# One program part instead of four for MLP, experts, graph rows and second attention of a two-layer graph network

## What is computed

```python
xn = layernorm(x)
# layer 0: weighted graph sum, linear attention with an MLP behind it, experts
x = x + segment_sum((xn @ W)[src] * edge_w, dst) + mix0(xn)       # mix0 ends: gelu(gelu(ln(a) @ w1 + b1) @ w2 + b2) + a
x = x + ffn0(layernorm(x))                                        # 8 experts of width 64, top 2 of a router
# layer 1
xn = layernorm(x)
h = (xn * rsqrt(mean(xn ** 2) + 1e-6) * rms_w) @ W_down           # 1024 -> 256
xl, xr = h @ Wl, h @ Wr                                           # 256 -> 256, 4 heads of 64
e = einsum(leaky_relu(xl[src] + xr[dst]), att)                    # a logit per edge and head
graph = segment_sum(segment_softmax(e, dst) * xl[src], dst) @ W_up
mix1 = (phi(q) (phi(k)^T v) / den) @ Wo + bo                      # q, k, v: 1024 -> 1024, 16 heads, 266 random features
x = x + graph + mix1
x = x + ffn1(layernorm(x))                                        # shared expert and 16 routed experts, top 2
```

## Time and profile before

| | |
|---|---|
| runs of the kernel before | 2126.6 us median of 3 (2124.15 to 2135.53) |
| profiled execution, its own time | 2126.32 us |
| span of its trace | 2124.5 us |
| TensorE busy | 1958.2 us (92%), 9370 products |
| VectorE, ScalarE, GpSimd busy | 740.6, 390.2, 640.6 us |
| mean granted TensorE clock | 0.958 of full |

### The profile page before, as it was taken

How to read it: one execution, slowest core, us unless ns; L and a number is a source line. 1 busy time by engine, 2 the same in 40 slices (tenths; PEclk the granted TensorE clock), 3 DMA queues, 4 the chain that set the end, 5 groups by cost and what they waited for, 6 DMA issues and landing times. The chain is left out here.

```text
span 2124.5 us, 23644 instructions
## 1 busy us (share of the span) xinstructions
PE 1958.2 (92%) x9370; PEld 1310.7 (62%) x9370; DVE 740.6 (35%) x1462; ACT 390.2 (18%) x726; POOL 640.6 (30%) x566
## 2 busy tenths in 40 slices
PE   7999999999997999999889999999979999999962
PEld 6475446456455676457667766677448778877841
DVE  5964103335044133544444552402101222122126
ACT  0000000012001010005557632110012211221112
POOL 0667840300000676777884000005100001001000
PEclk9999999999999999998999999999989999999986
DMA  9553141636100334332221441503137988888833
GB/s 352 141 141 66 2 99 41 206 69 263 46 0 15 114 97 127 91 79 59 52 57 18 105 123 40 201 18 119 40 129 281 353 335 331 349 351 320 343 96 103
DMA packets 111649, 306.58 MB, mean 144 GB/s; under 512 B 65892, under 2 KB 68575, under 8 KB 99423
## 3 DMA queue, kind: packets, MB, share of 16 engines
q1 hardware_dynamic: 29822, 224.82, 29.3%
q0 software_dynamic: 69840, 57.84, 11.5%
q10 hardware_dynamic: 11906, 22.80, 3.3%
HBM read 272.00 MB, written 32.94 MB: 144 GB/s over the span
## 5 line engine op out<-in xcount | busy, mean ns | idle before, releaser
L1882 PEld LDWEIGHTS bank<-picked_t,wring 128*128 128x128 f32 x2560 | 291.5, 193 | 10.3 <-issue 9.1
L1882 PE MATMUL bank<-picked_t,wring 128*128 128x128 f32 x2560 | 291.7, 276 | 0.8 <-DVE picked_t L1925 0.8
L326 PE MATMUL bank<-wring,ln_buf 128*125 128x512 f32 x480 | 207.6, 593 | 1.6 <-DVE ln_buf L630 0.7
L513 POOL DMA_INDIRECT table_d<-wring x85 | 173.0, 2036 | 107.6 <-issue 76.7
L326 PEld LDWEIGHTS bank<-wring,ln_buf 128*125 128x125 f32 x480 | 89.5, 188 | 115.3 <-issue 114.3
L1901 PE MATMUL bank<-wring,unit_t 128*128 128x512 f32 x320 | 148.0, 605 | 7.1 <-DVE unit_t L1931 7.1
L342 PE MATMUL bank<-x_buf,wring 128*128 128x312 f32 (+1 forms) x512 | 136.4, 429 | 13.7 <-PEq L962 13.7
L2108 POOL DMA_INDIRECT routed_d<-out_rows,place_of x20 | 19.8, 990 | 407.5 <-DVE out_rows L1952 407.5
L1085 POOL DMA_INDIRECT score_d<-wring x90 | 117.3, 1303 | 73.7 <-DMA score_d<-wring 52.3
L342 PEld LDWEIGHTS bank<-x_buf,wring 128*128 128x128 f32 x512 | 97.6, 191 | 52.5 <-issue 15.0
L1071 POOL DMA_INDIRECT wring<-xr_d,wring x85 | 116.2, 1367 | 25.9 <-issue 24.7
(11 more groups left out here) (360 smaller groups left out, 2865.2 us busy)
## 6 DMA issues: line engine op xcount, KB each, us to landing
wring<-in_experts SPq DMA_DIRECT2D x60, 2048.0 KB, 9.4
wring<-in_L_Ws SPq DMA_DIRECT2D x6, 2048.0 KB, 24.7
b_b<-in_expert_b ACTq DMA_DIRECT2D x22, 512.0 KB, 13.7
table_d<-eq_buf SPq DMA_DIRECT2D x2, 3072.0 KB, 29.5
score_d<-no_edge SPq DMA_DIRECT2D x2, 3072.0 KB, 31.0
wring<-table_d POOLq DMA_DIRECT2D x10, 610.4 KB, 7.3
wring<-score_d SPq DMA_DIRECT2D x5, 1093.8 KB
wring<-pid_d ACTq DMA_DIRECT2D x17, 312.5 KB
```

Of the source, the lines that this page charges most:

```text
L326: ins = pe.matmul(bank[0:R, :], act_t[:, k, tok(t)], w[:, k * HALF:(k + 1) * HALF], start=(k == 0), stop=(k == chunks - 1))
L513: pool.indirect_dma_start(out=tables_d[b % 2], out_offset=bass.IndirectOffsetOnAxis(ap=edge_at[:, b:b + 1], axis=0), in_=edge_sums[:, b, : ...
L1882: ins = pe.matmul(bank[:, c * BLK:(c + 1) * BLK], w[:, k * HALF + c * P:k * HALF + (c + 1) * P], picked_t[:, s, k, :], start=(k == 0), sto ...
```

## The change

One block takes the place of the four. With no block ends between them, buffers are shared by hand (`flat_b`, `flat_c`, `flat_d`, `turned_a`), and the router's small tensors lie in free columns of weight slot 5. No `pe_keep_busy` is left in this part. What differs inside:
- **Norms by tile.** `dve_tile_var`, `act_tile_root` and `dve_tile_norm` do one row tile each; `pe_turn` transposes one row tile (8 transposes to one bank of each ring). The first tiles are normed between the last MLP tiles, the others between gate-up tiles; in the graph rows' norm tile t is normed after the second down tile of t.
- **Experts.** silu reads the gate-up bank in PSUM, VectorE multiplies from PSUM (no `gu`); the hidden rows are turned by tile. The logits come after the third gate-up tile.
- **Graph rows.** Instead of `g_t`, the weights in slot 5 are scaled by `rms_w` (8 pieces of 256 columns, during the experts). The mean square comes from the variance already there. Wl and Wr come after the first of the four column chunks of q (`ends`), and `xlr` is stored with four DMAs, of 112 and of 13 partitions for each table.
- **Logits.** VectorE does groups 0 to 4 during q and k, 5 to 8 after values tiles 1, 4, 6, 9, then one group in 10.5 units of the loop (`LATE_STEP_AT`); group 17 falls behind the loop. The maxima of row tiles 0 and 1 come before the adds of the Wo tiles, and `TURN_AT`, `ROWS_AT`, `FIND_AT`, `WEIGH_AT` start one tile later.
- **Queues.** SyncE: after the MLP loads 13 to 16, the score table clear, load 17, a wait for the end of the gate-up product, edge ends and `att`, a wait for `xlr`, the four stores, the other loads. GpSimd: `rank` and `no_edge` before its adds of x; then waits for the clear and for the stores before its constants and the gathers. ScalarE: the load of `gate8` moves ahead of the MLP.

```diff
-        with nc.Block() as block:      # experts: L878 to L948
-                pe_keep_busy(pe, 30)
-                pe.wait_ge(normed.sem, normed.n + T)
-                pe_transposes(pe, rows)
-                pe_wait_evacuated(pe)
-                pe_logits(pe, x_t, gate8, NE0)
-                pe_gemm_rows(pe, x_t)
-                pe_keep_busy(pe, 28)
...
-        with nc.Block() as block:      # graph rows: L962 to L1025
-                pe_keep_busy(pe, 24)
...
-                sp.dma_start(xl_d.rearrange("(t p) d -> p t d", p=R), xlr[:, :, 0:HID]).then_inc(scratch_out, 16)
-                sp.dma_start(xr_d.rearrange("(t p) d -> p t d", p=R), xlr[:, :, HID:]).then_inc(scratch_out, 16)
...
+        tile_order.insert(tile_order.index(("mlp", 2 * T - 1)), ("turn", 0))
+        tile_order.append(("turn", 1))
...
+        def pe_turn(pe, src, t, ready):
+            pe.wait_ge(normed.sem, ready)
+            for g, ring in ((0, dring), (1, sring)):
+                bank = ring.produce(pe)
+                for j in range(4):
+                    ins = pe.transpose(bank[:, tok(j)], src[:, t, (4 * g + j) * P:(4 * g + j + 1) * P], ident[0:R, 0:R])
+                ins.then_inc(ring.filled, 1)
...
+        def dve_tile_var(v, t, eps):
+            after(v, dve_step)
+            dve_step.mark(v.bn_aggr(mv[:, t, :], stats[:, t, :, :].rearrange("p h s -> p (h s)")))
+            after(v, dve_step)
+            v.tensor_scalar(var_eps[:, t:t + 1], mv[:, t, 1:2], eps, None, ALU.add).then_inc(ln_var, 1)
...
+        def act_tile_root(s, t):
+            s.wait_ge(ln_var, act_calls[0])
+            s.activation(root[:, t:t + 1], var_eps[:, t:t + 1], ACT.Sqrt).then_inc(ln_root, 1)
...
-        QK_GROUPS = 6
-        LOOP_GROUP_AT = 6
+        QK_GROUPS = 5
+        V_GROUP_AT = {1: 5, 4: 6, 6: 7, 9: 8}
+        LATE_GROUP = QK_GROUPS + len(V_GROUP_AT)
+        LATE_STEP_AT = {6 + 21 * g // 2 + 2 * n for g in range(GROUPS_E + 1 - LATE_GROUP) for n in range(4)}
...
-        TURN_AT = {1: 0, 3: 1, 5: 2, 7: 3, 8: 4}
-        ROWS_AT = {3: 0, 5: 1, 7: 2, 8: 3, 9: 4}
-        FIND_AT = {1: 2, 2: 3, 4: 4}
-        WEIGH_AT = {0: 1, 3: 2, 5: 3, 7: 4}
+        TURN_AT = {2: 0, 4: 1, 6: 2, 7: 3, 8: 4}
+        ROWS_AT = {4: 0, 6: 1, 7: 2, 8: 3, 9: 4}
+        FIND_AT = {2: 2, 4: 3, 6: 4}
+        WEIGH_AT = {0: 0, 1: 1, 3: 2, 5: 3, 7: 4}
...
+            @block.tensor              # gate-up in the one block
+                for h in range(2):
+                    w = wt.take(pe)
+                    for t in range(T):
+                        if h == 0:
+                            pe_wait_turned(pe, turned[t])
...
+                        if (h, t) == (0, 0):
+                            turned[2] = pe_turn(pe, rows, 2, LN_FFN + 3)
+                            turned[3] = pe_turn(pe, rows, 3, LN_FFN + 4)
+                        if (h, t) == (0, 1):
+                            turned[4] = pe_turn(pe, rows, 4, LN_FFN + 5)
+                        if (h, t) == (0, 2):
+                            pe_wait_turned(pe, turned[4])
+                            pe_logits(pe, x_t, gate8, NE0)
+                        if h and t:
+                            turn_hidden(t - 1)
...
+                pe_gemm_cols(pe, x1_t, ring=sring, beside=ends)
...
+            @block.vector              # last MLP tiles
+                    if n >= T + 2:
+                        dve_tile_norm(v, res, rows, n - T - 2, calls[n - T - 2])
+                    if n >= 1:
+                        add_output(n - 1)
+                    if n >= T + 1:
+                        calls[n - T - 1] = dve_tile_var(v, n - T - 1, 1e-5)
...
-                    if u >= LOOP_GROUP_AT and u % 2 == 0:
+                    if u in LATE_STEP_AT:
                         next(late, None)
-                    if TOP_AT <= u < TOP_AT + 2 * GH:
-                        find_top((u - TOP_AT) // GH, (u - TOP_AT) % GH)
-                assert next(late, "none") == "none"
+                for _ in late:
+                    pass
                 v.wait_ge(hsem["o_copied"], HEADS)
...
-                weigh(0)
+                find_tops(0)
+                find_tops(1)
...
+            @block.sync
+                sp.wait_ge(d_emptied, xlr_made[0])
+                for r0, n in ((0, 112), (112, R - 112)):
+                    for table, at in ((xl_d, 0), (xr_d, HID)):
+                        sp.dma_start(table.rearrange("(t p) d -> p t d", p=R)[r0:r0 + n],
+                                     xlr[r0:r0 + n, :, at:at + HID]).then_inc(scratch_out, 16)
```

More of the change, by code:

```diff
@@ new lines, in _ @@
+                mid_tiles = sring.made
+                turned = {}
+                for kind, n in tile_order:
+                    if kind == "agg":
+                        agg_tile(n)
+                        continue
+                    if kind == "turn":
+                        turned[n] = pe_turn(pe, rows, n, LN_FFN + n + 1)
+                        continue
+                    if n == 0:
+                        pe.wait_ge(s_emptied, mid_tiles)
+                    h, t = n // T, n % T
+                    bank = dring.produce(pe)
+                    pe.matmul(bank[0:R, :], mid_t[:, tok(t)], w[:, D + h * HALF:D + (h + 1) * HALF],
+                              start=True, stop=True).then_inc(d_filled, 1)
+                    if n == 2 * T - 1:
+                        wt.free(dring.filled, dring.made)
@@ new lines, in _ @@
+                w = wt.take(pe)
+                for h in range(2):
+                    for t in range(T):
+                        if h == 0:
+                            pe.wait_ge(s_emptied, turned["hidden", t])
+                        bank = dring.produce(pe)
+                        for k in range(4):
+                            ins = pe.matmul(bank[0:R, :], x_t[:, k, tok(t)],
+                                            w[:, k * D + h * HALF:k * D + (h + 1) * HALF],
+                                            start=(k == 0), stop=(k == 3))
+                        ins.then_inc(d_filled, 1)
+                        if (h, t) == (0, 0):
+                            turn_hidden(T - 1)
+                        if h and t == T - 1:
+                            wt.free(dring.filled, dring.made)
+                        if h and t:
+                            turned["gnn", t - 1] = pe_turn(pe, rows1, t - 1, LN_GNN + t)
@@ new lines, in _ @@
+                made = [multiply_up(0, 0)]
+                keep_turned_rows(v, dring, 0, x_t, 2, copy)
+                keep_turned_rows(v, dring, 0, x_t, 3, copy)
+                made.append(multiply_up(1, 0))
+                keep_turned_rows(v, dring, 0, x_t, 4, copy)
+                made.append(multiply_up(2, 0))
+                v.wait_ge(rank_made, 1)
+                dve_top2(v, router, NE0, 1)
+                dve_step.mark(v.tensor_reduce(router.sum[:], router.w[:], AX.X, ALU.add))
@@ new lines, in _ @@
+                after(v, dve_step)
+                dve_step.mark(v.reciprocal(router.sum[:], router.sum[:]))
+                after(v, dve_step)
+                dve_step.mark(v.tensor_tensor(router.w[:], router.w[:],
+                                              router.sum[:].unsqueeze(2).to_broadcast([R, T, NE0]), ALU.mult))
+                after(v, dve_step)
+                for t in range(3):
+                    weigh_hidden(t, 0, made[t])
+                v.wait_ge(wt.loaded[5], 16 * (wt.loads(5, GNN_LOAD) + 1))
@@ new lines, in _ @@
+                dve_step.mark(v.tensor_tensor(var_eps[:], var_eps[:], mv[:, :, 1], ALU.mult))
+                after(v, dve_step)
+                v.tensor_scalar(var_eps[:], var_eps[:], 1e-6, None, ALU.add).then_inc(ln_var, 1)
+                ln_calls[0] += 1
+                v.wait_ge(ln_root, ln_calls[0])
+                dve_step.mark(v.reciprocal(rstd[:], root[:]))
+                after(v, dve_step)
+                for t in range(T):
+                    v.tensor_scalar(xlr[:, t, :], dring.consume(v)[0:R, :], rstd[:, t:t + 1], None, ALU.mult)\
+                        .then_inc(d_emptied, 1)
```

631 lines of the change are left out of this document (330 added, 301 removed).

## The result

| | before | changed |
|---|---|---|
| runs | 2126.93 us median of 4 (2124.15 to 2135.53) | 2064.41 us median of 4 (2062.34 to 2066.19) |
| profiled execution, its span | 2126.32, 2124.5 us | 2065.79, 2063.9 us |
| TensorE busy | 1958.2 us, 9370 products | 1918.0 us, 9206 products |
| VectorE, ScalarE, GpSimd busy | 740.6, 390.2, 640.6 us | 728.1, 400.9, 631.4 us |

The ratio is 0.9702, 95% interval 0.9677 to 0.9728: 62.5 us less. Forecast were 67 us less, 2059 us. "Changed" means the first of them unless it is said otherwise.

The account below looks back on a forecast made before the run. TensorE was held by block ends with norms over all tiles and by GpSimd's gather pace. 46 + 17 + 29 - 25 = 67 us less, 2126.3 - 67 = 2059 us; range 2036 to 2092.

Parts of the forecast that it names:

- Part 1: One block, 494 to 832 us: TensorE's products of ones and idle before products go, 46 us less.
- Removed: 21.6: Products of ones that nobody reads, between MLP and values: 21.6 us, counted in full among 46.5 us removed.
- Switching tables: ScalarE alternating gelu and square root in the last MLP tiles: 3.4 us a tile, under VectorE's 3.7, costing nothing.
- Part 2: Values stage: TensorE no longer waits behind logits whose gathers are late, 17 us less; first gather near 665.
- Part 3: The loop: 64 units at 2.353 us without waits for gathers, 29 us less.
- Part 4: Behind the loop: late logits and scores make TensorE wait 18.6 us before the first turn; 25 us more in all.
- The last ten scatters can only start when group 16's logits are made, E - 2: Behind the loop: logits hold GpSimd's last scatters, the last issued at E + 24, scores loaded from E + 26.6.
- E: The loop's end, when the last output is copied, forecast at 1112 us.
- No new wait: Rival, behind the loop: the graph's scores are ready when TensorE asks; 2037 us, chance 0.13.
- GpSimd still sets the loop: Rival, in the loop: GpSimd's gathers get slower beside VectorE and the loop waits again; 2074 to 2088 us, chance 0.15.
- Norms in the open: Rival, in the block: norms by tile stand in the open, giving back 12 us rather than 2; 2069 us, chance 0.12.
- The two outer ones: Rivals: little done, saved time only moves to the scores, 2124 us; slower, much slower gathers, 2157 us; chance 0.04 each.

Follow-up runs that it names:

- before_no_busywork: The kernel before without its three runs of products of ones (30, 28, 24) between the MLP's end and the values: 2129.66 us, ratio 1.001.
- old_schedule: The changed kernel with the schedule of the graph's logits, turns and maxima as before; block, norms by tile and stores stay changed: 2089.97 us, ratio 0.9823.
- stores_of_125: The changed kernel with one store of 125 partitions per table of graph rows, in place of 112 + 13: 2056.69 us, ratio 0.9672.
- second profile: The changed kernel itself, nothing altered, measured and profiled again in a later sitting: 2055.62 us, ratio 0.9666.

## Why the prediction was right

- **Part 1, 46 forecast, 51.8 measured.** The gap ahead of gate-up was the one named ("3 us after the MLP now ends"): 498.37, with 0.5 us of idle. Mis-sized was what the old stages cost beside their large waits: 0.8 + 0.7 + 0.6 us in three small groups of the same view that the sum left out (below), and 1.4 us in the query product (135.0 for 136.4). The 2 us given back were 1.2 (idle 0.5 and 0.7). That is 4.3 of the 5.8 us; the rest is spread.

```profile
L354 PE MATMUL bank<-wring,x_t 128*125 128x512 f32 x80 | 34.6, 593 | 0.8 <-DVE x_t L925 0.8
...
L831 PE MATMUL bank<-gate,x_t 128*125 128x100 f32 x80 | 8.9, 273 | 0.7 <-DVE x_t L902 0.7
...
L985 PE MATMUL bank<-wring,down_t 128*125 128x256 f32 x40 | 8.9, 382 | 0.6 <-DVE down_t L1004 0.6
```

- **The step "Removed: 21.6".** Right in the sum, and `before_no_busywork` shows how it had to be read: alone it gives nothing (+2.6 us).
- **Switching tables.** ScalarE in the last MLP tiles:

```profile
495.75 1.28 ACT L845 ACT_TABLE_LOAD   x1
497.05 0.20 ACT L845 ACTIVATE root<-var_eps 125x1 f32<-125x1 f32 x1
...
497.75 1.28 ACT L1550 ACT_TABLE_LOAD   x1
499.04 0.63 ACT L1550 ACTIVATE flat_c<-flat_c 125x512 f32<-125x512 f32 x1
```

  A load takes 1.28 us and the activation follows at once, again and again in the last tiles. The drain of 1.38 us that the Trainium skill gives (ScalarE: Activation LUTs, What ACT_TABLE_LOAD costs) is not there, and gate-up starts with 0.5 us of idle.
- **Part 2, 17 forecast, 16.0 measured.** The first gather at 663.10 was forecast near 665. The schedule was needed for it as well: with the old one 24.7 us of idle stand in the values although GpSimd starts at 661.53 (`old_schedule`). How much of the earlier start is needed no run shows; at group 5 the changed kernel has 6.5 us between last gather and logits, and a start 5.4 us later (`stores_of_125`) did no harm.
- **Part 3, 29 forecast, 22.2 measured,** and in the second profile 1103.99 - 881.28 = 222.7 against 253.7, which is 31. "64 units at 2.353" was right; the 7 us missing in the first measurement are its slow units, which nothing in rows 1 to 13 could show.
- **Part 4, 25 forecast, 30.0 measured.** The wait was named with its place and price (18.6; it was 23.5). The step that failed is "The last ten scatters can only start when group 16's logits are made, E - 2". With E = 1113.86 the last ten began at 1113.07, 1.9 us after group 16's logits, so the time of the last scatter came out near by luck (1141.35, E + 27.5 for E + 24). Two runs with earlier logits brought no earlier scores: the bound is GpSimd's own chain, whose last 20 scatters wait for one another for 60 us. The trace of before had it already (17.2 us between group 16's logits and its first scatter).
- **Two sums in part 4.** From 1128.91 to 1172.60 there are fifteen scatters, not sixteen, so their distance is 43.7 / 14 = 3.12 us and not 2.91, and the last ten end at E + 26.1 (they took 28.3 us, 3.14 each). And the terms behind E + 26.6 (7, 4.9, 5.3, 4.1 and an add) give E + 48.6, not E + 50. Measured, the score load was at E + 30.1, the first diagonals at E + 55; on the way the load took 7.6 us for 7, and VectorE makes the maxima of both row tiles ahead of the first diagonals, the second of them 2.4 us late for its scores. TensorE reached the wait at E + 31.5, as forecast (31.4).
- **The rivals.** "No new wait" is out (23.5 us). "GpSimd still sets the loop" is out for the changed kernel: no step of the loop waits for a gather, and GpSimd's gathers did not get slower beside VectorE's work (from 700 to 1060 us a mean of 1.22 and 1.29 us for the two tables, 1.24 and 1.36 before). It describes the kernel with the old schedule, 2090 us. It also came back in another place: GpSimd sets the scores. "Norms in the open": 0.5 us. The two outer ones had no place.
- The 5 us by which 2059 lies below 2064.4 are within what the same kernel differs by between sittings (2055.6, 2058.8, 2064.4). The closeness is in part luck: part 1 gave 5.8 us more than forecast, parts 2 to 4 together 12.8 less.

## What to carry to other kernels

Where engine work is moved so that its consumer never waits, ask who used that wait: with the graph's logits out of the way of the loop, a wait of 23 us came back at the first reader of the scores, and two more tiles of work ahead of that reader won 11.7 us. Products that only fill a wait are worth nothing to remove and something to cover: count the chain that they stand beside. And before blaming the last producer, move it: here the logits came 9.7 us earlier and the scores did not, because a chain of transfers, each waiting for the landing of the last, was the bound.

## What the runs showed of the hardware

- The same program ran its loop at 2.33 us a unit in two sittings and took 8.8 us more in another, with 15 units of 2.6 to 3.2 us, where both other engines waited 0.64 us longer for TensorE's product at a granted clock of 1.00. Within a sitting its four runs agree within 0.3%, between sittings, on different chips, its medians differ by 0.4%.
- After 6.9 us of idle TensorE's products were nearly as slow as after 23.6 (7.29 and 7.63 us for 40 records, 4.53 at full clock), after 12.9 us a little less so (6.04), and 16.9 us of products ahead of a wait of 7.4 did not keep the clock: it was 0.69 in the 10 us around the first turn, 0.68 without them.
- Right behind two transfers of 640 KB on SyncE's queue two of GpSimd's chained scatters followed the one before at 6.5 and 6.0 us (6.6 and 6.0 in a second run); the last three of the changed kernel are 2.85 us apart.
